# A low-pass block on one core: output matmuls cut into 64-row halves, and steps made twice as long

## The reference

```
xs = einsum('bhwc,dc->bhwd', x, W1) + b1      # x: 16 x 64 x 64 x 768, D = 192
xs = gelu(xs, approximate=False)
xs = fft_low(xs)                              # per image and channel, over h and w
xs = einsum('bhwd,cd->bhwc', xs, W2) + b2
return x + xs

def fft_low(x):
    fft = fftshift(fft2(x, norm='forward')) * mask      # a square of low frequencies stays
    return abs(ifft2(ifftshift(fft), norm='forward').real)
```

## Time and profile before

| | |
|---|---|
| median of 2 runs | 2202.78 us (2202.62 to 2202.95) |
| profiled execution | 2201.8 us; its span, first to last instruction, 2200.0 us |
| PE busy | 97% of the span |
| PEld, DVE, ACT, POOL | 88%, 74%, 51%, 15% |
| transfers, share of the 16 DMA engines | 86.1% |
| granted TensorE clock | 0.998 of full speed |

### The profile page before, as it was taken

The page is one execution under the profiler, slowest core; times in us unless marked ns, Lnnn a source line. Parts: engine busy times, 40 slices in busy tenths (PEclk is TensorE's granted clock), DMA queues, the critical chain, the costliest instruction groups (busy, mean ns, idle before and its releaser), DMA issues.

```text
span 2200.0 us, 37824 instructions
## 1 busy us (share of the span) xinstructions
PE 2142.0 (97%) x12512; PEld 1939.0 (88%) x12512; DVE 1623.7 (74%) x2380; ACT 1114.4 (51%) x1861; POOL 327.5 (15%) x500
## 2 busy tenths in 40 slices
PE   6899999999999999999999999999999999999998
PEld 5799988989899898988989889998898989989876
DVE  6768687686877868778686776868768687786846
ACT  4565454645445555454554546545464544555532
POOL 1311111111111111111111111111111111111100
PEclk9999999999999999999999999999999999999999
DMA  6789988898888988988889888998889889888878
GB/s 209 234 304 350 347 316 306 322 361 335 302 325 322 345 322 314 344 317 329 333 319 350 316 320 318 351 344 314 305 322 363 332 293 334 325 342 324 317 291 344
DMA packets 253758, 707.40 MB, mean 322 GB/s; under 512 B 84242, under 2 KB 150930, under 8 KB 249620
## 3 DMA queue, kind: packets, MB, share of 16 engines
q1 hardware_dynamic: 253716, 706.86, 86.1%
HBM read 455.12 MB, written 251.66 MB: 321 GB/s over the span
## 4 chain that ended last, share of the span: by engine, by line
PE 92%; ACT 3%; DVE 2%; issue 1%; DMA 1%; SPq 0%; DVEq 0%; ACTq 0%
PE ps_h L277 24%; PE ps_h L278 11%; PE ps_o L341 8%; PE ps_o L338 8%; PE ps_o L335 8%; PE ps_o L332 8%; PE ps_o L331 8%; PE ps_o L316 8%; PE ps_f L288 2%; PE ps_o L310 2%; PE ps_f L290 2%; PE ps_f L289 2%; DVE xlo L464 1%; ACT xhi L372 1%; DMA rows_b<-filt 1%
## 5 line engine op out<-in xcount | busy, mean ns | idle before, releaser
L277 PE MATMUL ps_h<-w1s,xhi 128*128 128x384 f32 x3072 | 899.7, 361 | 25.0 <-DVE xlo L464 24.3
L278 PE MATMUL ps_h<-w1s,xlo 128*128 128x192 f32 x3072 | 770.9, 251 | 0.0
L277 PEld LDWEIGHTS ps_h<-w1s,xhi 128*128 128x128 f32 x3072 | 579.2, 189 | 42.5 <-DVE xlo L464 17.7
L511 DVE TENSOR_TENSOR xo<-ps_o,xo 128x1024 f32<-128x1024 f32 x384 | 470.3, 1225 | 178.5 <-PE ps_o L341 174.5
L278 PEld LDWEIGHTS ps_h<-w1s,xlo 128*128 128x128 f32 x3072 | 588.7, 192 | 7.6
L390 ACT ACTIVATE filt<-ps_f 128x384 f32<-128x384 f32 x256 | 126.2, 493 | 799.6 <-PE ps_f L290 799.2
L464 DVE TENSOR_TENSOR xlo<-xin,xhi 128x1536 fp32r<-128x1536 f32 x256 | 450.4, 1759 | 3.9 <-ACT xhi L372 3.9
L575 POOL TENSOR_TENSOR diff<-hid 128x192 f32<-128x192 f32 x240 | 166.8, 695 | 1462.6 <-ACT hid L381 1460.6
L372 ACT ACTIVATE xhi<-xin 128x1536 fp32r<-128x1536 f32 x256 | 377.8, 1476 | 8.2 <-DMA xin<-xt_dram 7.9
L473 DVE TENSOR_TENSOR hid<-ps_h,b_rows 128x192 f32<-128x192 f32 x512 | 181.0, 354 | 185.4 <-PE ps_h L278 183.1
L341 PE MATMUL ps_o<-ob,w2b_hi 128*128 128x512 f32 x768 | 303.4, 395 | 1.0 <-DVE ob L502 1.0
(11 more groups left out here) (52 smaller groups left out, 2056.6 us busy)
## 6 DMA issues: line engine op xcount, KB each, us to landing
xin<-xt_dram SPq DMA_DIRECT2D x256, 768.0 KB, 7.3
xo<-xt_dram SPq DMA_DIRECT2D x128, 1536.0 KB, 12.2
out_dram<-xo SPq DMA_DIRECT2D x128, 1536.0 KB, 8.6
rows_a<-filt SPq DMA_DIRECT2D x256, 128.0 KB, 5.2
cols_a<-rows_a SPq DMA_DIRECT2D x64, 512.0 KB, 3.7
rows_b<-filt SPq DMA_DIRECT2D x256, 64.0 KB, 6.2
cols_b<-rows_b SPq DMA_DIRECT2D x64, 256.0 KB, 4.2
xo<-w1t_dram SPq DMA_DIRECT2D x1, 576.0 KB, 4.5
```

Of the source, the lines that this page charges most:

```text
L277: nc.tensor.matmul(ps_h[tt][:, 0:2 * D], hi, w1s[:, k, :], start=k == 0, stop=False)
L278: ins = nc.tensor.matmul(ps_h[tt][:, D:2 * D], lo, w1s[:, k, 0:D], start=False, stop=k == KC - 1)
L511: nc.vector.tensor_tensor(x, ps_o[u % 2][:].rearrange("p (j a n) -> p j a n", j=2, a=2), x, ALU.add).then_inc(s_add, 1)
```

## The change

The kernel is written over in five places.

* Channels are cut into three blocks of 64 (`BLOCKS`). A row pair of the image is stacked: partitions 0 to 63 hold a block for one half of the tokens, partitions 64 to 127 for the other half. `rows_a`/`rows_b` become one tensor `rows`, `cols_a`/`cols_b` one tile `cols`, `ya`/`yb` one tile `y`.
* An output unit is now 128 output channels by 1024 tokens, again two banks. For each of the three blocks and three products there are two matmuls of 64 rows by 512 columns: one on partitions 0 to 63 that writes the first bank, one on partitions 64 to 127 that writes the second. W2 is held twice, on both halves of the partitions. b2 is added by DVE (`scalar_tensor_tensor` with `b2_cols`).
* Two pairs make one step (`DSTEPS` = 8). TensorE does the first half of two pairs, then, in steps 0 and 1, six banks of the filter along h, and in steps 2 to 7 four output units one after another.
* The residual comes in a layout of its own, `xr`, in 24 transfers of 512 KB an image, with 12 slots; the output goes out in 24 transfers of 512 KB.
* A pair's filtered rows are written in four transfers (two tiles by two partition parities) with runs of 64 channels.

TensorE's code for an image is written out in full in the loop over images: 974 matmuls where there were 782, each with its weight load, and with the register and wait instructions 2041 instructions where there were 1674.

```diff
-            def out_unit(i, u):
-                g, jp = divmod(u, UPG)
-                r = g % 2
-                if u < 2:
-                    pe.wait_ge(s_yev, BANKS * (i + 1))
-                else:
-                    pe.wait_ge(s_add, UNITS * i + u - 1)
-                for jj in range(2):
-                    o = ps_o[u % 2][:, 512 * jj:512 * (jj + 1)]
-                    ...
-                    nc.tensor.matmul(o, w2a_hi[:, c], oa_hi[:, r, :], start=True, stop=False)
-                    ...
-                    ins = nc.tensor.matmul(o, w2b_hi[:, c], ob[:, r, :], start=False, stop=True)
-                ins.then_inc(s_o, 1)
+            def out_unit(i, g, q, u):
+                k, r = u % KC, u // KC
+                c = slice(k * P, (k + 1) * P)
+                if u < 2:
+                    pe.wait_ge(s_yev, BANKS * (i + 1))
+                if past(g, 2):
+                    pe.wait_ge(s_add, g - 1)
+                for w, x in ((w2_hi, y_hi), (w2_lo, y_hi), (w2_hi, y_lo)):
+                    if k == 0 and w is w2_hi:
+                        pe.wait_ge(s_yhi if x is y_hi else s_ylo, q + 1)
+                    for j in range(BLOCKS):
+                        for v in range(2):
+                            h = slice(v * DB, (v + 1) * DB)
+                            ins = nc.tensor.matmul(bank(2 * (u % 2) + v), w[h, j, c], x[h, r, j, :],
+                                                   start=x is y_hi and w is w2_hi and j == 0, stop=x is y_lo and j == BLOCKS - 1)
+                ins.then_inc(s_o, 1)
...
+            def multiply(i, d, a, n):
+                p = HEAD + 2 * d
+                for m in range(2):
+                    ...
+                        mm1(PAIRS * i + p + m, m)
+                    ...
+                        filter_w_pair(PAIRS * i + p + m - 1, 1 - m)
...
+            def turn(i, a, c, n):
+                for d in range(FIRST_O):
+                    multiply(i, d, a, n)
+                    if c:
+                        for b in range(BANKS_PER):
+                            y_bank(i - 1, BANKS_PER * d + b)
+                for j in range(ROUNDS):
+                    output_round(i, j, a, c, n)
+                if a:
+                    corner_sums(i)
```

The queue of SP in a step, and the write of the rows:

```diff
             def turn(i, a, c, n):
-                for s in range(STEPS):
-                    m = s + HEAD
-                    if a and s in READ_AT:
-                        read_cols(i, READ_AT.index(s))
...
+                for d in range(DSTEPS):
+                    p = HEAD + 2 * d
+                    if a and d in READ_AT and READ_AT[d] < 3:
+                        read_cols(i, READ_AT[d])
+                    for m in range(2):
+                        if (x := pair_at(i, p + X_AHEAD + m, a, n)) is not None:
+                            load_x(*x)
+                    if c:
+                        for u in units_at(d - 1):
+                            store(i - 1, u)
+                        for u in units_at(d + 1):
+                            load_xo(i - 1, u)
+                    if (f := pair_at(i, p - 1, a, n)) is not None:
+                        write_rows(*f)
+                    if a and d == DSTEPS - 1:
+                        read_cols(i, HGROUPS - 1)
+                    if (f := pair_at(i, p, a, n)) is not None:
+                        write_rows(*f)
```

More of the change, by code:

```diff
@@ L17, with lowpass_kernel @@
 TOKENS = 2 * P
-GROUPS = PAIRS // 2
-GTOK = 2 * TOKENS
+GROUPS = 4
+GTOK = TILES * P // GROUPS
+NTOK = GTOK // 2
 HEAD = 2
-STEPS = PAIRS
+DSTEPS = PAIRS // 2
 X_SLOTS = 4
[L25 to L34, removed]
-OBANKS = 4
[L37 to L40, removed]
+X_AHEAD = 4
+XO_SLOTS = 12
+BLOCKS = D // DB
+MCOLS = W // 4
+YBANKS = BLOCKS
+BANKS = MCOLS // 4 * YBANKS
+BANKS_PER = BANKS // 2
+OBANKS = 4
+UNITS = GROUPS * KC
+FIRST_O = 2
+O_PER = 4
+SPLIT_AT = {1: 0, 2: 1, 3: 2, 5: 3}
+ROUNDS = 2
+PER_ROUND = (DSTEPS - FIRST_O) // ROUNDS
 HGROUPS = 4
 ROWS_PER = H // HGROUPS
[L45 to L50, removed]
+READ_AT = {2: 0, 4: 1, 6: 2, 7: 3}
+def lowpass_kernel(nc, xt, xr, w1t, b1, w2t, b2, filter_w, filter_h, corner_in, corner_out, out):
+    rows = nc.dram_tensor("rows", (H, 2, MCOLS, BLOCKS, 2, DB), F32, kind="Internal").ap()
     ctx = ExitStack()
@@ L279, in mm1_pair, with filter_w_pair @@
                     ins.then_inc(s_m1, 1)
-            def filter_w_pair(i, q):
-                if q == 0 and not later(i):
+            def filter_w_pair(g, b):
+                if not past(g, 1):
                     pe.wait_ge(s_setup, 1)
-                pe.wait_ge(s_hlo, PAIRS * i + q + 1)
-                if q >= 1 or later(i):
-                    pe.wait_ge(s_fs, PAIRS * i + q)
-                hi, lo = (m[:, q % 2, :, :].rearrange("p t d -> p (t d)") for m in (hid_hi, hid_lo))
+                pe.wait_ge(s_hlo, g + 1)
+                if past(g, 1):
+                    pe.wait_ge(s_fs, g)
+                hi, lo = (m[:, b, :, :].rearrange("p t d -> p (t d)") for m in (hid_hi, hid_lo))
                 nc.tensor.matmul(ps_f[:, 0:2 * D], fw_hi[:], hi, start=True, stop=False)
@@ L319, in out_unit @@
-            def out_unit(i, u):
-                g, jp = divmod(u, UPG)
-                r = g % 2
+                if b >= OBANKS:
+                    pe.wait_ge(s_yev, BANKS * i + b - OBANKS + 1)
+                c, j = divmod(b, YBANKS)
+                o = bank(b)
+                nc.tensor.matmul(o, corner[:, j, :], corner_hw[:], start=True, stop=False)
+                for m in range(4):
+                    ins = nc.tensor.matmul(o[:, m * P:(m + 1) * P], cols[:, 4 * c + m, j, :], fh[:], start=False, stop=m == 3)
@@ L554, in turn @@
                     if units:
                         add_unit(i - 1, units[0])
-                    if here is not None:
-                        hid_lo_pair(*here)
-                    if a and s == STEPS - 1:
-                        corner_split(i)
+                    if here[1] is not None:
+                        hid_lo_pair(*here[1])
+                    if units:
+                        add_unit(i - 1, units[1])
+                    if units and ahead[1] is not None:
+                        xlo_pair(*ahead[1])
@@ L560, in turn @@
+                    if units:
+                        add_unit(i - 1, units[2])
+                    if c and d in SPLIT_AT:
+                        split_lo(i - 1, SPLIT_AT[d])
+                if a:
+                    corner_split(i)
                 if c:
```

349 lines of the change are left out of this document (137 added, 212 removed).

## The result

The changed kernel takes 2314.23 us (2310.16 to 2318.3) where the kernel before takes 2202.78: a ratio of 1.051, with an interval of 1.049 to 1.053. It is slower by 5%, and above the range of the forecast. The profiled execution took 2318.3 us, its span 2315.9; the granted clock was 0.963 of full speed over the span, 0.998 before.

A forecast was written before the change was run, and what follows sets the result against it. PE was taken to bound the kernel, with transfers second. From 2201.8 us, -89.5 (output), +35 (switches), -6 (first turn) and +7 gave 2148, so 2149 us at the median, ratio 0.976; range 2080 to 2280 us.

The forecast's parts named there:

- The output: Output matmuls on PE: two half-height matmuls run side by side at 0.233 us a pair, -89.5 us in all.
- The switches: PE changing between 128 and 64 rows twelve times an image: 0.18 us each, +35 us (bounds 0 and +70).
- The first turn: Turn without outputs, a chain of ACT, DVE and PE: two pairs a step save 6 us (bounds -17 and 0).
- the wait for units two back: In a double step, unit n waits for unit n-2's addition on DVE: put among terms that cost nothing.
- The wait for `hid_lo`: PE's wait before the second pair's `filter_w_pair`: left as it was, 1.3 us an image.
- the code's 7 us: Term for TensorE's loop code in the sum: +7 us on the profiled execution.
- the queue of transfers: Rival: rows stand last in SP's queue in double steps 3 to 6 and land late; 2277 us, chance 0.12.
- the code: Rival: TensorE's loop code no longer stays and is loaded once a pass; 68 us, total 2210 us, chance 0.04.
- a landing above 16 us: Sign of the queue rival: `rows` landing above 16 us, or PE waiting for ACT's `filt`.
- Over a whole image 44 MB need 118 of 131 us: Argument against the queue rival: an image's transfers need less time than the image takes.
- steps 0, 1 and 7 can take up a backlog: Argument against the queue rival: these double steps can absorb transfers delayed in double steps 3 to 6.
- The price of 64 us for each us late: Queue rival: each us of row landing beyond 16.6 us costs 4 double steps x 16 = 64 us.

The follow-up runs named there:

- both cures: Changed kernel with TensorE's output steps in an inner loop and only half of each output unit stored: 2130.08 us.
- half stores: Changed kernel with only the first half of each output unit stored, same issues and order: 2201.92 us, 0.999.
- the three that move all bytes: Changed kernel with inner loop and stores issued on POOL, 2133.11 us; inner loop and SP's other order, 2141.66; image loop written out and that order, 2144.71.
- inner loop: Changed kernel with TensorE's output steps in an inner loop of two rounds in images 2 to 14: 2202.42 us, 0.9997.
- written out: Changed kernel with TensorE's image loop written out, so its code never branches back: 2249.15 us, 1.022.
- SP's other order: Changed kernel with SP issuing, per double step, first pair's rows, stores, second pair's rows, then residual loads: 2256.57 us, 1.024.
- the run with longer runs: Changed kernel with inner loop, row writes in runs of 768 B instead of three of 256 B: 2166.3 us, 0.983.

## Why the prediction was wrong

**What held.** The output: 0.229 us a pair, 0.233 forecast. The switches and the turn as a whole: 130.4 us where nothing is in the way, 131 forecast. The first turn: 5 us less, 6 forecast. Of the terms put at nothing, the wait for units two back cost at most 3.2 us in all. The wait for `hid_lo`, which was left at 1.3 us an image, is gone where the rows are early, and a new one for DVE's `hid` on `ps_h` (15 to 18 us in all, 0.7 before) stands in its place: that these two nearly cancel is luck. The sum without the code's 7 us, 2142, lies 12 us above the kernel with both cures and half stores (2130) and beside the three that move all bytes (2133, 2142, 2145).

**The step that failed: the sum put the code at 7 us and the queue of transfers at nothing, and both losses happened at once.** As rivals they were weighed as exclusive, with chances of 0.12 for the queue and 0.04 for the code. What each cost, by what was cured (medians in us):

| | body loaded in each pass | inner loop | written out |
|---|---|---|---|
| rows late | 2314 | 2202 | 2249 |
| SP's other order | 2257 | 2142 | 2145 |
| half stores | 2202 | 2130 | not run |

The code costs 65 to 115 us and the rows 58 to 112, depending on what else is cured; the two together 169 to 184. They do not simply add: a branch back costs 6.0 us with half stores and 9.4 with SP's other order, and the rows cost more or less with the way the code is reached. Why the one changes the price of the other was not found.

*Code.* The term "0.5 us a pass, 7 us" should have been 65 us or more; its upper bound of 68 lies at the low end of what was measured, and it got a chance of 0.04. The 5.2 us behind that bound were the landing of a row write, not a load, and came near by luck. The term was argued from the kernel before, whose code stays. But 25 packets for 1674 instructions told nothing of 2041, and 1770 are already too many. The price of a branch back is two waits, together 3.1 us in the pass shown and 8.4 in the one with SP's other order, and a piece at half the clock behind them; the sum had no term for the clock after a stall. A pass that is reached straight on pays nothing, so 12 passes pay, not 13.

*The queue.* The mechanism is the rival's: a slot that is held longer than a double step of 16.6 us. The profile has 21.6 us in the step shown, and the stall, 5.33 us, is about the excess. But the 21.6 us are not made up as the rival reckoned. It had the rows land 16.4 to 20.6 us after their issue, and named a landing above 16 us as its sign; the write shown lands 11.72 us after its issue, and the median of all row writes is 4.7, less than the 5.2 before. The other 9.9 us pass on SP: 5.9 until it comes to the first of the four writes, and 4.0 from there to the fourth.

Two things made the rival too cheap. "Over a whole image 44 MB need 118 of 131 us" took the rate of the kernel before; in the changed kernel they need 125, and the run with longer runs takes 4.9 of that away. In the kernel with the rows on ACT's queue the rows took 230 us for 50.4 MB, where the other transfers' rate would give 136. And "steps 0, 1 and 7 can take up a backlog" does not help in the steps between, where it grows: from the copy into the slot to the landing of its last row write it takes 4.7 us for pair 1, 12.0 for pair 7, 16.8 for pair 9 and 21.3 for pair 13 (means over the images 3 to 14). The price of 64 us for each us late, for four double steps an image, was too high for the same reason. One step an image stalls: PE waits 66.5 us for `hid_lo` in all, and with the low clock behind the stalls the rows cost 58 to 112 us.

**Which cause of the late rows.** Issue count as such is out (half stores, as many issues). Bytes, short runs and order are one cause seen from three sides: the queue is so full that what stands last in it comes late. Longer runs take away about half of the loss, fewer bytes or another order all of it. Order suffices alone, so the bandwidth is there. What stays open is how much of the lateness is SP's own time: its 1024 row issues take 933 us in the changed kernel, 740 with half stores and 714 with the inner loop and the other order, so they are held up where the queue is full, and no run changes one without the other.

## What to carry to other kernels

When a change makes the bounding engine faster, ask of every transfer on a shared queue what stands ahead of it and how long its buffer can be held; an average of 90% DMA time says nothing of the one that stands last. Count the instructions of a loop body against one that is known to stay: a body written out in full cost 65 to 115 us here, where an inner loop costs nothing that shows (turns of 130.4 us with it, 130.5 with all code written out straight), and two losses found in one trace should be cured together before the change itself is judged.

## What the runs showed of the hardware

* Two matmuls of 64 rows by 512 columns on the two halves of the partitions, each with its own weight load, take 0.229 us together, less than one of 128 rows (0.233).
* A loop body on TensorE of 1674 instructions stays, one of some 1770 is loaded again after each branch back. The 2048 that the Trainium skill gives (Runtime: NRT & Kernel Launch, Instruction fetch mechanics) is more than these runs allow for a loop body.
* A branch back to code that has gone makes PE wait 3.6 us (half stores), 4.1 us (the changed kernel) or 6.3 us (SP's other order) on average of 12 branches, and a branch costs 4.4 to 9.4 us a turn (4.4 and 5.7 with 12 and 25 added waits in the kernel before, 6.0 with half stores, 9.4 with SP's other order). Code that runs straight on is loaded without any wait (124 packets, turns of 130.5 us).
* Behind the 5.33 us stall of PE the granted clock was 0.50 from 1085 to 1089 us. The filter and the three groups of six matmuls behind it took 5.26 us (1085.86 to 1091.12) where they take 2.82 without a stall ahead (996.62 to 999.44), so the stall cost 2.4 us more.
* Four issues of 48 KB in 256-byte runs hold the issuing ACT for 3.0 us.
